# A decoder of six parts: ScalarE's order in the last stage set by kind of slot, and GpSimd's scalars of eight cut into eight pieces

## The reference

```python
x = x + _L0_attn_ref(_layernorm(x), ...)          # causal attention, 16 heads of 8
x = x + _L0_xattn_ref(_layernorm(x), ctx, ...)    # attention to 77 context rows, 16 heads of 64
x = x + _L0_ffn_ref(_layernorm(x), ...)           # best 2 of 8 gated experts
x = x + _L1_attn_ref(_layernorm(x), ...)          # att = softmax over heads: axis=3 of 'nqhd,nkhd->nhqk'
x = x + _L1_xattn_ref(_layernorm(x), ctx, ctx, ...)   # see below
x = x + _L1_ffn_ref(_layernorm(x), ...)           # best 2 of 4 unlike experts
```

```python
# fifth: temperature per sequence and head from three numbers of its own scores
feats = [scores.mean(), scores.max(-1).mean(), var(softmax(scores), ddof=1).mean()]
t = exp(clip(linear(gelu(linear(gelu(linear(feats)))))))
out = softmax(qk / (2 * t)) @ V                       # then Wo, bo
# sixth: rw, sel = top_k(x @ router_w + router_b + load_balancer, 2); rw = softmax(rw)
e0 = silu(x @ sw_w1) * (x @ sw_w3) @ sw_w2
e1 = gelu(((x @ me_eq_w + b) @ me_wv + b) @ me_wo + b  @ me_c1w + b) @ me_c2w + b
e2 = norm(h2 + relu(h2 @ ce_f1w + b) @ ce_f2w + b) @ ce_gen_w + b   # h2 = norm(syn + attn)
e3 = gelu(x @ ml_w1 + b) @ ml_w2 + b
out = sum over the 2 chosen of rw * expert
```

## Time and profile before

| | |
|---|---|
| median of three runs | 3006.04 us |
| the profiled execution, its own time | 3000.5 us |
| its span | 2998.7 us |
| busy: TensorE, VectorE, ScalarE, GpSimd | 2706.9, 2100.0, 1909.6, 1942.5 us |
| granted TensorE clock, mean | 0.959 |
| eight slots of the over-heads attention | 51.40 us |
| four slots of the last stage | 53.67 us |

### The profile page before, as it was taken

How to read it: one execution, slowest core, us unless ns; L and a number is a source line. 1 busy time by engine, 2 the same in 40 slices (tenths; PEclk the granted TensorE clock), 3 DMA queues, 4 the chain that set the end, 5 groups by cost and what they waited for, 6 DMA issues and landing times. The chain is left out here.

```text
span 2998.7 us, 82306 instructions
## 1 busy us (share of the span) xinstructions
PE 2706.9 (90%) x27846; PEld 2305.6 (77%) x27847; DVE 2100.0 (70%) x4559; ACT 1909.6 (64%) x4300; POOL 1942.5 (65%) x3245
## 2 busy tenths in 40 slices
PE   7999987999999999499997999985899999999996
PEld 6788766888888888399985888873677777777775
DVE  4677655677667676456657999987777878878643
ACT  3666545666666666355554777774877877778762
POOL 4566544566566666426668989875667877768652
PEclk9999998999999999699998999995899999999998
DMA  8666530000000000223331000000000000000000
GB/s 236 180 185 189 172 113 20 2 10 13 13 12 12 14 12 13 72 74 88 89 84 44 0 0 0 0 1 0 2 5 5 5 8 5 9 5 5 8 5 11
DMA packets 204792, 129.08 MB, mean 43 GB/s; under 512 B 13840, under 2 KB 197112, under 8 KB 203896
## 3 DMA queue, kind: packets, MB, share of 16 engines
q1 hardware_dynamic: 196344, 108.80, 12.2%
q0 software_dynamic: 8192, 16.79, 1.9%
HBM read 35.05 MB, written 90.51 MB: 42 GB/s over the span
## 5 line engine op out<-in xcount | busy, mean ns | idle before, releaser
L1575 PE MATMUL a_ps_s<-a_qk,w_ident 128*128 128x256 f32 x1024 | 238.6, 387 | 20.2 <-POOL a_qk L1682 19.1
L1013 POOL TENSOR_TENSOR x_p<-x_p,x_rz 128x1232 f32<-128x1232 f32 x64 | 143.9, 2248 | 169.1 <-DVE x_rz L1122 168.0
L635 DVE TENSOR_REDUCE a_nmax<-a_ps_s 128x4 f32<-128x512 f32 x256 | 165.0, 686 | 110.1 <-PE a_ps_s L381 106.4
L1682 POOL TENSOR_TENSOR a_qk<-a_qkv 128x2048 f32<-128x2048 f32 x64 | 235.4, 3678 | 2.6 <-POOL a_eight L218 1.0
L479 ACT ACTIVATE a_e<-a_ps_s 128x512 f32<-128x512 f32 x256 | 139.0, 595 | 148.0 <-PE a_ps_s L386 148.0
L1575 PEld LDWEIGHTS a_ps_s<-a_qk,w_ident 128*128 128x128 f32 x1024 | 192.2, 193 | 50.2 <-POOL a_qk L1682 22.7
L2401 POOL TENSOR_TENSOR x_sq<-x_e 128x1232 f32<-128x1232 f32 x64 | 143.2, 2238 | 125.3 <-DVE x_t_sq L2560 125.2
L1656 ACT ACTIVATE a_r<-a_o,w_a_rows 128x128 f32<-128x128 f32 x512 | 220.5, 521 | 1.7 <-DVE a_o L1741 1.7
L1411 POOL DMA_INDIRECT f_yg<-f_rows_out,f_index x120 | 114.9, 958 | 132.2 <-DVE f_yo L1490 111.9
L895 ACT ACTIVATE x_uu_hi<-x_ps_u 128x308 fp32r<-128x308 f32 x256 | 101.9, 423 | 111.3 <-PE x_ps_u L758 111.1
L1129 DVE TENSOR_REDUCE x_top<-x_ps_s 128x16 f32<-128x1232 f32 x64 | 91.2, 1425 | 112.0 <-PE x_ps_s L758 112.0
(11 more groups left out here) (626 smaller groups left out, 9642.1 us busy)
## 6 DMA issues: line engine op xcount, KB each, us to landing
f_rows_in<-a_zeros SPq DMA_DIRECT2D x31, 1088.0 KB, 5.4
f_rows_out<-a_zeros SPq DMA_DIRECT2D x31, 1088.0 KB, 8.8
f_xin<-f_rows_in SPq DMA_DIRECT2D x135, 64.0 KB
f_rows_out<-f_yo SPq DMA_DIRECT2D x135, 64.0 KB, 1.6
out<-x SPq DMA_DIRECT2D x16, 256.0 KB, 2.3
f_raw<-in_late_f SPq DMA_DIRECT2D x2, 1408.0 KB, 6.2
w_ctx<-in_ctx SPq DMA_DIRECT2D x1, 2464.0 KB
f_rows_in<-f_xr,f_where POOLq DMA_INDIRECT x128, 2.3
```

The lines of the kernel that those rows point to most:

```text
L635: nc.vector.tensor_reduce(nmax[:, u % 2, g, :], ps_s[g][:, :].rearrange("p (t k) -> p t k", t=GROUP), AX.X, ALU.max, negate=True).then_inc ...
L1013: nc.gpsimd.tensor_tensor(wide, wide, rz[:, :].unsqueeze(2).broadcast_to([P, HEADS, K]), ALU.mult).then_inc(p_ready, 1)
L1575: ins = nc.tensor.matmul(ps_s[u % 2][:, 0:HEADS * HEADS], c.ident[:, :], qk[:, u % 2, k, :, :], start=k == 0, stop=k == HD - 1)
L1682: nc.gpsimd.tensor_tensor(qk[:, u % 2, :, :, :], qkv[:, u % UNROLL, 0, :, :].unsqueeze(3).broadcast_to(full), qkv[:, u % UNROLL, 1, :, :]. ...
```

## The change

In `scalars_of` the four parts become eight; the instructions are the same, and in the same order. `self_attention` and the two late calls take them as before in four calls (`QUARTERS`), except that one multiplication (`rate`) goes a slot earlier where there is a shift. The over-heads attention calls one piece in each of its eight slots. In the last stage ScalarE's order at the start of a slot follows the kind of slot, two one-column activations (`warm`) are added that cause a table load ahead of its use, and in MIXED the experts' piece goes ahead of the small network's, on TensorE and on ScalarE.

```diff
+QUARTERS = ((0, 1, 2), (3,), (4, 5), (6, 7))
-def scalars_of(..., begun, parts=(0, 1, 2, 3)):
+def scalars_of(..., begun, parts=tuple(range(8))):
     if 0 in parts:
         nc.gpsimd.tensor_tensor(both, me, mo, ALU.add)
         nc.gpsimd.tensor_tensor(dif, me, mo, ALU.subtract)
         after(nc.gpsimd.tensor_tensor(sq, ve, vo, ALU.add))
+    if 1 in parts:
+        n[0] = 1
         nc.gpsimd.tensor_tensor(mean, both, half, ALU.mult)
         after(nc.gpsimd.tensor_tensor(dif2, dif, dif, ALU.mult))
+    if 2 in parts:
+        n[0] = 2
         after(nc.gpsimd.tensor_scalar(wide, dif2, D / 4, None, ALU.mult))
...
-    if 1 in parts:
+    if 3 in parts:
         n[0] = 6 if second else 5
         rough_root(vpe)
-    if 2 in parts:
+    if 4 in parts:
         n[0] = 7 if second else 6
-        newton_terms(vpe)
+        newton_terms(vpe, (0, 1))
+    if 5 in parts:
+        n[0] = 9 if second else 8
+        newton_terms(vpe, (2,))
+        last = nc.gpsimd.tensor_tensor(rate, square, rough, ALU.mult)
...
-                if (at := sl.step(LAST + 1)) and (at[1] + 1) % EIGHT < 4:
+                if at := sl.step(LAST + 1):
...
                 if (k := gated(t)) is not None:
                     tempering(k, n)
-                if (j := tile(t, MIXED)) is not None:
-                    mixing(j, n)
# mixing now stands ahead of tempering (TensorE); likewise on ScalarE the Gelus of MIXED stand ahead of L2255 to L2261
...
-                if spread is not None:
-                    act.wait_ge(dg_ready, spread + 1)
-                    nc.scalar.activation(d[...], d[...], ACT.Exp, scale=0.5).then_inc(p_ready, 1)
+                early = tile(t, GATED) is not None or tile(t, MIXED) is not None
+                late = tile(t, TURNED) is not None or tile(t, OPENED) is not None
+                def tempered(): ...     # the lines taken out above
+                def weighed(): ...      # the Exp x_e with its three waits, as before
+                if tile(t, TURNED) is not None:
+                    nc.scalar.activation(warm[:, 0:1], c.ident[:, 0:1], ACT.Exp)
+                else:
+                    tempered()
+                if early:
+                    weighed()
+                if tile(t, GATED) is not None:
+                    nc.scalar.activation(warm[:, 1:2], c.ident[:, 0:1], ACT.Silu)
                 if (s := step(t, TURN)) is not None:
                     act.wait_ge(xT_ps, s + 1)
                     nc.scalar.activation(xT[:, s % 2, :], ps_x, ACT.Copy).then_inc(xT_ready, 1)
+                if tile(t, TURNED) is not None:
+                    tempered()
                 if (j := tile(t, OPENED)) is not None:
                     ...                 # x_xm, as before
-                if (s := step(t, WEIGH)) is not None:
-                    ...
+                if not early and not late:
+                    weighed()
                 experts(t, 1)
                 ...                     # qT, kT, v
                 experts(t, 2)
+                if late:
+                    weighed()
```

More of the change, by code:

```diff
@@ L173, in scalars_of_four, with scalars_of @@
     scalars_of(c, pool, own, done, s, 4, st, second, shift, s if begun is None else begun)
-def scalars_of(c, pool, own, done, s, group, st, second, shift, begun, parts=(0, 1, 2, 3)):
+def scalars_of(c, pool, own, done, s, group, st, second, shift, begun, parts=tuple(range(8))):
     nc = c.nc
@@ L198, in rough_root, with newton_terms @@
         after(nc.gpsimd.tensor_tensor(rough, x, minus_half, ALU.pow))
-    def newton_terms(x):
-        after(nc.gpsimd.tensor_tensor(square, rough, rough, ALU.mult))
-        after(nc.gpsimd.tensor_tensor(dif, square, x, ALU.mult))
-        after(nc.gpsimd.tensor_scalar(square, dif, -0.5, 1.5, ALU.mult, ALU.add))
+    def newton_terms(x, some):
+        if 0 in some:
+            after(nc.gpsimd.tensor_tensor(square, rough, rough, ALU.mult))
+        if 1 in some:
+            after(nc.gpsimd.tensor_tensor(dif, square, x, ALU.mult))
+        if 2 in some:
+            after(nc.gpsimd.tensor_scalar(square, dif, -0.5, 1.5, ALU.mult, ALU.add))
     if 0 in parts:
@@ L218, in scalars_of @@
             after(nc.gpsimd.tensor_scalar(vpe, dif2, 1.0 / D, EPS, ALU.mult, ALU.add))
-    if 1 in parts:
+    if 3 in parts:
         n[0] = 6 if second else 5
         rough_root(vpe)
-    if 2 in parts:
+    if 4 in parts:
         n[0] = 7 if second else 6
-        newton_terms(vpe)
+        newton_terms(vpe, (0, 1))
[3 more added lines that the diff above has]
+        last = nc.gpsimd.tensor_tensor(rate, square, rough, ALU.mult)
+        if second or shift:
+            after(last)
         if second:
-            after(nc.gpsimd.tensor_tensor(rate, square, rough, ALU.mult))
             after(nc.gpsimd.tensor_tensor(sq, rate, rate, ALU.mult))
@@ L229, in scalars_of @@
             after(nc.gpsimd.tensor_scalar(vpe, dif2, EPS, None, ALU.add))
-    if 3 in parts:
+    if 6 in parts and second:
+        n[0] = 14
+        rough_root(vpe)
+        newton_terms(vpe, (0, 1, 2))
+    if 6 in parts and shift and not second:
+        n[0] = 10
+        nc.gpsimd.tensor_tensor(rstd, rate, c.powers[:, 3, 0:group], ALU.mult)
+        after(nc.gpsimd.tensor_tensor(again, mean, rate, ALU.mult))
+    if 7 in parts:
+        n[0] = 18 if second else steps
         if second:
-            n[0] = 14
-            rough_root(vpe)
-            newton_terms(vpe)
             after(nc.gpsimd.tensor_tensor(again, square, rough, ALU.mult))
             last = nc.gpsimd.tensor_tensor(rstd, rate, again, ALU.mult)
-        else:
-            n[0] = 9
-            last = nc.gpsimd.tensor_tensor(rate, square, rough, ALU.mult)
-            if shift:
-                after(last)
-                nc.gpsimd.tensor_tensor(rstd, rate, c.powers[:, 3, 0:group], ALU.mult)
-                after(nc.gpsimd.tensor_tensor(again, mean, rate, ALU.mult))
-                last = nc.gpsimd.tensor_tensor(shifts, again, minus_one, ALU.mult)
-        assert n[0] == steps, n
+        elif shift:
+            last = nc.gpsimd.tensor_tensor(shifts, again, minus_one, ALU.mult)
         last.then_inc(done, group)
@@ L2140, in experts @@
                     closing(j, n)
+                if (j := tile(t, MIXED)) is not None:
+                    mixing(j, n)
                 if (k := gated(t)) is not None:
                     tempering(k, n)
-                if (j := tile(t, MIXED)) is not None:
-                    mixing(j, n)
             nc.tensor.matmul(ps_o[:, 0:D], c.w["x1_bv"][:, :], c.w["x1_o"][:, :], start=True, stop=True).then_inc(b_ps, 1)
@@ L2252, in experts @@
                     nc.scalar.activation(ex, dif[:, :, :], ACT.Exp).then_inc(h_filled, 1)
+                if (j := tile(t, MIXED)) is not None and n in (1, 2):
+                    act.wait_ge(*filled("me", j, n - 1))
+                    nc.scalar.activation(hid[3 + n], bank, ACT.Gelu, bias=c.f1_me_b[:, n - 1:n]).then_inc(h_emptied, 1)
+                if (j := tile(t, MIXED)) is not None and n in (3, 4, 5, 6):
+                    act.wait_ge(*filled("ml", j, n - 3))
+                    nc.scalar.activation(hid[n - 3], bank, ACT.Gelu, bias=f["ml_b1"][:, n - 3:n - 2]).then_inc(h_emptied, 1)
                 if (k := gated(t)) is not None and n == 3:
@@ L2261, in experts @@
                     nc.scalar.activation(h2[:, :], ps_h2, ACT.Gelu, bias=c.w["x1_mlp_b"][:, 1:2]).then_inc(d_emptied, 1)
-                if (j := tile(t, MIXED)) is not None and n in (1, 2):
-                    act.wait_ge(*filled("me", j, n - 1))
-                    nc.scalar.activation(hid[3 + n], bank, ACT.Gelu, bias=c.f1_me_b[:, n - 1:n]).then_inc(h_emptied, 1)
-                if (j := tile(t, MIXED)) is not None and n in (3, 4, 5, 6):
-                    act.wait_ge(*filled("ml", j, n - 3))
-                    nc.scalar.activation(hid[n - 3], bank, ACT.Gelu, bias=f["ml_b1"][:, n - 3:n - 2]).then_inc(h_emptied, 1)
             act.wait_ge(made, 1)
```

26 lines of the change are left out of this document (16 added, 10 removed).

## The result

The changed kernel takes 2985.48 us, median of 8 runs (2982.07 to 2992.78), against 3004.55 (2996.42 to 3013.29, 8 runs) of the kernel before beside it: ratio 0.9939, 95% interval 0.9924 to 0.9953, which is 18.3 us or 0.61% faster (the two medians lie 19.1 apart). The forecast was 2980. The profiled execution takes 2985.8 us (span 2984.0), against 3000.5.

The account below looks back on a forecast made before the run. TensorE was taken to bound both stages, so gains come from its idle time: 7 us over heads plus 18.5 in the last stage, 25.5 in all, from the median of 3006.0 to 2980.5 us; range 2960 to 2999.

Parts of the forecast that it names:

- The bound in the last stage: Last stage: GpSimd's chain to `x_full` becomes the new bound, so each period gains 1.26 us; forecast case, chance 0.50.
- The 1.13 of MIXED: MIXED: with `x_e` moved into ScalarE's wait, the Gelu and TensorE's second product come 1.13 us earlier.
- the short stop: OPENED: `x_qT` overtakes the projections and ScalarE stops briefly, so `x_m_hi` comes about 1.04 us earlier, not 1.13.
- TensorE's new waits: Last stage, per period: the rest of TensorE's idle time becomes waits of about 1.2 us for `x_full`, 0.6 for `x_d`.
- The price 0 for the small network's place: MIXED: putting the small network behind the products neither gains nor costs; the load waiting for its last layer isn't late.
- TURNED and OPENED: TURNED's copy passes `x_d`, so TensorE's 1.30 us wait nearly goes; in OPENED `x_e` behind `x_v` removes 0.43.
- GATED: GATED: `x_e`, the table load and `warm`, 2.65 us together, fit ScalarE's wait of 2.80 by 0.15.
- Rival D, the ring through `x_e`: TURNED: `x_e` comes too late and delays VectorE's sum and GpSimd's square; slower, 3013 us, chance 0.06.
- The ends of the stage: Last stage's ends: four thinner periods gain 2.0 us, and the Exp's load in the last two tiles 2.6.
- The 2.6 for the Exp's load: Last two tiles: `warm` moves the Exp's load (1.28 us) out of the chain into idle time, gaining 2.6 us.
- Over heads: Over-heads attention: spreading GpSimd's scalars gains 1.0 us a burst, seven bursts, 7 us; VectorE is late next.
- the sign I named: Over heads: eight slots in 50.4 us and TensorE's waits for `a_qk` under 0.6 us a burst.

Follow-up runs that it names:

- 4: Changed kernel without both one-column activations (`warm`): ratio 0.9953 to the kernel before, last-stage period 53.25 us.
- 9: Changed kernel with `x_e` in TURNED back ahead of the second `x_hT`: ratio 0.9940 to the kernel before, period 52.63 us.
- 10: Changed kernel without the one-column Silu activation in GATED, the Exp one kept: ratio 0.9938 to the kernel before, period 52.53 us.
- 5: Kernel before with `x_e` ahead of the copy in GATED and MIXED, plus the eight pieces over heads: ratio 0.9950, period 53.34 us.
- 8: Kernel before with `x_e` early in GATED and MIXED, small network behind MIXED's work, eight pieces over heads; no `warm`: ratio 0.9934, period 52.43 us.
- experiment 6: Kernel before with only TURNED's and OPENED's edits (Exp `warm` included) in the last stage, plus eight pieces over heads: ratio 0.9979, period 53.57 us.
- experiment 7: Changed kernel with two 16-bit buffers for GpSimd's squares: ratio 0.9881 to the kernel before, period 52.14 us.
- experiment 11: Changed kernel with two 16-bit square buffers and VectorE's sums a slot later from OPENED on: ratio 0.9898 to the kernel before, period 52.14 us.
- experiment 1: Kernel before with only the eight pieces over heads; last stage and `rate` elsewhere as before: ratio 0.9995.
- 2: Kernel before with only the last stage's new order, `scalars_of` and its calls as before: ratio 0.9951, period 52.63 us.
- 3: Kernel before with only `rate` made a slot earlier, four parts over heads and the last stage as before: ratio 1.0007.
- experiment 1's repeat: Second run of the kernel before with only the eight pieces over heads: ratio 0.9989.

## Why the prediction was right, and where it was not

*The bound in the last stage: right.* The 1.13 of MIXED arrives as 1.06, `x_xm` is stopped by `x_mom` (by 0.19; I had `x_mom` done 0.2 ahead of it), the square and the norms follow `x_m_hi`, the product of `x_full` closes its slack of 0.22. The sum said 1.26 and it is 1.13; the 0.16 short is between `x_xm` and `x_m_hi`, where I had 1.04. There `x_xm` gained 1.21 and `x_m_hi` 0.88. It is the short stop that I had priced at 0.09: with `x_e` behind `x_v` in OPENED, `x_qT` waits 0.21 for TensorE's projections, and `x_m_hi` follows `x_xm` by 4.43 to 4.45 us (after, 4, 9, 10), where it was 4.11 to 4.13 (before, 5, 8). This is also why the period of experiment 8 is the shorter one. TensorE's new waits are 0.84 for `x_full` (1.2 said) and 0.86 for `x_d` (0.6 said). Experiments 6 and 8 show the link: a wait of 1.3 for ScalarE can go or stay with the period moving by no more than 0.1. Experiments 7 and 11 show how far it reaches: loosened, it gives 0.4, and then something else binds.

*The price 0 for the small network's place: wrong.* It is worth 0.91 a period (experiments 5 and 8), since it lets the Gelu's gain through. It was in the change, so the sum didn't suffer; as a working it was luck. I had asked whether the moved work would be late, not whether, left in place, it would stop TensorE.

*TURNED and OPENED: the mechanism right, the credit wrong.* I said that TensorE's wait for the copy "would nearly go" and that `x_full` would take its place; both hold. But then these edits could not be part of what gains: alone they give 0.1 (experiment 6), beside the others they cost 0.1 (8 against the changed kernel), and they need the Exp `warm` (0.7) to do no harm.

*GATED: fits, by 0.17 where I said 0.15.* The row of the load behind `x_e` and `warm` stands above: 1.29 from load to `warm`. The Trainium skill's figure of 2.66 us for a switch ("ScalarE: Activation LUTs", section "What ACT_TABLE_LOAD costs") would not have fitted into the wait; the trace doesn't agree with it. But whether it fits decides nothing (experiment 10).

*Rival D, the ring through `x_e`:* not there; moving `x_e` to the front again gains nothing (experiment 9).

*The ends of the stage: 4.6 said, and 4.1 by other parts, which is luck.* From one `x_m_lo` to the next, ten full periods gave 11.1 us and the eleventh 1.0, where I had 13.9. The other 4.1 of the 16.2 come so. Up to the first `x_m_lo` the stage took 125.3 us, against 127.9: 2.7 that no edit made, since experiment 1, whose last stage is the old one, has 125.3 too. The first period fell from 54.17 to 50.80, 3.4 us, for which I had no term. In eight of nine profiles with `x_e` early it took 49.9 to 51.5, at a clock of 0.97 or more, and 54.2 to 55.2 in the five without, at 0.88 to 0.91; but in experiment 11, which has it early, 53.7 at 0.92. Behind the eleventh period 2.0 were lost.

The 2.6 for the Exp's load, my largest term there, was wrong. `warm` takes the load out of its old place, behind `x_ff`, but not out of the chain: it stands there again, ahead of the first `x_hT`, in both last tiles. The chain that ended last, after (before: the earlier trace rows):

```profile
2893.94 1.28 ACT L2310
2895.24 0.20 ACT x_warm L2310
...
2939.99 1.28 ACT L2310
2941.29 0.20 ACT x_warm L2310
```

What it gains there is only that the load now runs beside TensorE's transposes: from a tile's last Silu to the end of its second `x_ff` it took 6.49 and 6.32 us before, and 5.73 and 5.56 after. That is 0.76 twice, 1.5 us and not 2.6.

In this execution the clock took it back. The stretch between the last two tiles' `x_m_lo`, before and after, columns as in the earlier trace rows:

```profile
2895.20:2936.66 41.46, 32.59 (x228) 25.32 (x226) 17.50 (x57) 19.14 (x33) 17.86 (x43) 1.00 0.02 7
```
```profile
2878.86:2923.49 44.63, 36.56 (x228) 28.59 (x226) 17.51 (x57) 19.34 (x35) 17.85 (x43) 0.89 0.02 7
```

The same 228 matmuls, but the granted clock is 1.00 in one and 0.89 in the other. The same sixteen products, before and after:

```profile
2931.01 2.05 PE L2045 MATMUL x_ps_h<-w_f_f,x_ff 128*128 128x128 f32 x16 [0.78 <-ACT x_hid L2267]
```
```profile
2915.11 3.78 PE L2058 MATMUL x_ps_h<-w_f_f,x_ff 128*128 128x128 f32 x16 [0.78 <-ACT x_hid L2271]
```

In both kernels TensorE stood still for some 0.8 us ahead of each group of three products there; in one the clock held at the higher level, in the other it fell to the lower (a stretch with 0.50, from 2912.70 to 2918.60 in the kernel after). Over all the profiles: with TURNED and OPENED as changed (after and experiments 2, 4, 6, 7, 9, 10, 11) this stretch took 43.0 to 44.9 us, eight times out of eight; without (before and 1, 3, 5, 8) it took 41.4 to 41.5 in five of six, and 43.1 once, in experiment 1's repeat, with a clock of 0.96. So those edits go with some 3 us more in this stretch, by the clock, which can fall without them too. From the last `x_m_lo` to the end it is the other way round: 55.3 to 60.6 us with them and 59.5 to 62.4 without, at clocks of 0.79 to 0.96. The two stretches together take 98.3 to 105.4 us with them and 100.9 to 105.4 without (105.1 after, 103.5 before). The low clock comes at other places in other executions, and a cost of these edits in the whole tail is not shown. Why the clock falls where it does was not tried.

*Over heads: right, but not by the sign I named.* I said 1.0 a burst; it is 0.81, and 7 us in all, of which 4.4 are left at the stage's end. What I left out is that GpSimd's product can come earlier without the stage ending earlier: VectorE's `a_ev`, the bound, gained 4.3 from first to last (experiment 1). I said that TensorE's waits for `a_qk` fall under 0.6 a burst; they are 10.3 us in 17 waits, 1.9 a burst, where it was 11.0 in 10, now spread, and none over 0.8. What binds is VectorE, as said: its slots in the kernel after are 6.50, 6.34, 6.23 and so on, which add up to the 50.59, with no wait but 0.2 of issue:

```profile
1753.64 2.27 DVE L1739 TENSOR_TENSOR a_ev<-a_ps_e,a_qkv 128x2048 f32<-128x2048 f32 x1
...
1760.14 2.29 DVE L1739 TENSOR_TENSOR a_ev<-a_ps_e,a_qkv 128x2048 f32<-128x2048 f32 x1 [0.20 <-issue]
...
1766.48 2.28 DVE L1739 TENSOR_TENSOR a_ev<-a_ps_e,a_qkv 128x2048 f32<-128x2048 f32 x1
```

In sum: 7 + 18.5 said. The traces have 4.4 + 16.2, of which at least 2.7 is variation, and 5.8 of variation the other way ahead of both; the times, 18.3 in all. Over heads the times of the pieces alone, 0 to 5 us, agree with the 4.4.

A version faster than the changed kernel is experiment 7, 0.9881 against 0.9939, with squares rounded to 16 bits; of that difference the periods explain some 4 us. Experiment 8's order with two squares was not tried.

## What to carry to other kernels

Measure a periodic schedule from one instruction of its bound, not by its waits: the distance of each step from it shows at which step a gain stops. An engine that isn't the bound is a bad yardstick: GpSimd's product told 6.8 us over heads where the stage gained 4.4. A wait that an edit removes is worth nothing where the work behind it waits for another engine next, and an edit priced at nothing may be the one that lets the others through. Undo the parts one by one, and leave out what brings nothing; here half of the edits did.
